# Second cross attention: the softmax matrix turned by VectorE blocks and device memory in place of TensorE

## The reference, cut to what matters

```python
def _L1_xattn_ref(query, key, value, w_q, w_k, w_v, w_o):   # key = value = ctx_1024 (8, 1024, 256)
    q = (query @ w_q).reshape(B, Q, HEADS, HEAD_DIM).transpose(0, 2, 1, 3)
    k = (key @ w_k)...; v = (value @ w_v)...
    scores = jnp.einsum('bhqd,bhkd->bhqk', q, k) * scale
    attn = jax.nn.softmax(scores, axis=-1)
    out = jnp.einsum('bhqk,bhkd->bhqd', attn, v)
    return out.transpose(0, 2, 1, 3).reshape(B, Q, HEADS * HEAD_DIM) @ w_o
x = x + _L1_xattn_ref(_layernorm(x, axis=-1), ctx_1024, ctx_1024, ...)
```

## Time and profile before

| what | us |
|---|---|
| median of 3 runs | 1009.84 |
| profiled execution, span from first to last instruction | 1008.6 |
| the stage changed (main loop and its tail) | 424 to 866 |
| one batch of 8 pairs in it | 52 |
| PE busy over the whole span | 963.9 |
| DVE, ACT, POOL busy over the whole span | 552.4, 497.9, 180.9 |

### The profile page before, as it was taken

How to read it: one execution, slowest core, us unless ns; L and a number is a source line. 1 busy time by engine, 2 the same in 40 slices (tenths; PEclk the granted TensorE clock), 3 DMA queues, 4 the chain that set the end, 5 groups by cost and what they waited for, 6 DMA issues and landing times. The chain is left out here.

```text
span 1008.6 us, 21010 instructions
## 1 busy us (share of the span) xinstructions
PE 963.9 (96%) x8772; PEld 798.4 (79%) x8772; DVE 552.4 (55%) x800; ACT 497.9 (49%) x716; POOL 180.9 (18%) x188
## 2 busy tenths in 40 slices
PE   8999999888899999899999999999999999997997
PEld 7888887665689985589999999998989996657554
DVE  5677777666443354565646465646464642367212
ACT  4777776353656645554444454454444532321331
POOL 2000000022224423012121212121212101421101
PEclk9999999899989999999999999999999999999999
DMA  5211110022023304111111111111113000599994
GB/s 154 86 47 47 47 47 5 2 63 65 2 84 94 94 22 167 37 48 43 43 43 42 42 42 42 42 42 42 42 58 140 0 1 1 133 332 310 336 328 143
DMA packets 57366, 84.55 MB, mean 84 GB/s; under 512 B 5506, under 2 KB 46163, under 8 KB 57299
## 3 DMA queue, kind: packets, MB, share of 16 engines
q1 hardware_dynamic: 56466, 81.22, 25.5%
q0 software_dynamic: 832, 2.36, 0.8%
HBM read 80.94 MB, written 2.62 MB: 83 GB/s over the span
## 5 line engine op out<-in xcount | busy, mean ns | idle before, releaser
L186 PE MATMUL ps<-f_pT_hi,f_cN_hi 128*128 128x256 f32 x512 | 145.4, 284 | 0.0
L186 PE MATMUL ps<-f_pT_hi,f_cN_lo 128*128 128x256 f32 x512 | 144.7, 283 | 0.0
L186 PE MATMUL ps<-f_pT_lo,f_cN_hi 128*128 128x256 f32 x512 | 144.7, 283 | 0.0
L1596 ACT ACTIVATE e_pr<-ps,e_negmax 128x1024 f32<-128x1024 f32 x64 | 71.5, 1116 | 129.9 <-DVE e_negmax L1601 127.6
L1870 DVE TENSOR_TENSOR f_pT_lo<-ps,f_pT_hi 128x1024 fp32r<-128x1024 f32 x64 | 78.3, 1224 | 81.8 <-ACT f_pT_hi L1808 81.6
L186 PE MATMUL ps<-e_cT_hi,e_qb_hi 128*128 128x512 f32 (+1 forms) x288 | 115.4, 401 | 0.0
L186 PE MATMUL ps<-e_cT_hi,e_qb_lo 128*128 128x512 f32 (+1 forms) x288 | 109.8, 381 | 0.0
L186 PE MATMUL ps<-e_cT_lo,e_qb_hi 128*128 128x512 f32 (+1 forms) x288 | 109.1, 379 | 0.0
L1808 ACT CAST f_pT_hi<-ps 128x1024 fp32r<-128x1024 f32 x64 | 64.9, 1014 | 84.6 <-PE ps L1920 83.8
L445 DVE SCALAR_TENSOR_TENSOR a_u<-ps,a_floor,a_cap 128x1024 f32<-128x1024 f32 x64 | 79.2, 1279 | 48.3 <-PE ps L540 47.9
L186 PEld LDWEIGHTS ps<-f_pT_hi,f_cN_hi 128*128 128x128 f32 x512 | 97.8, 191 | 2.6 <-issue 0.8
(11 more groups left out here) (401 smaller groups left out, 1961.0 us busy)
## 6 DMA issues: line engine op xcount, KB each, us to landing
k_w<-in_L_ffn_W SPq DMA_DIRECT2D x30, 1024.0 KB, 13.3
a_ctxT<-in_ctxT SPq DMA_DIRECT2D x16, 512.0 KB, 4.5
d_w<-in_L_ffn_w SPq DMA_DIRECT2D x32, 256.0 KB, 2.7
e_raw<-in_ctxT SPq DMA_DIRECT2D x8, 1024.0 KB, 5.0
e_raw<-in_ctx SPq DMA_DIRECT2D x8, 1024.0 KB, 5.8
k_b<-in_L_ffn_b SPq DMA_DIRECT2D x14, 256.0 KB, 11.8
k_w<-in_L_xattn_w_q SPq DMA_DIRECT2D x1, 1024.0 KB, 5.1
e_wk<-in_L_xattn_w_k SPq DMA_DIRECT2D x1, 1024.0 KB, 7.6
```

Of the source, the lines that this page charges most:

```text
L186: last = nc.tensor.matmul(out, a[i], b[j], start=start and n == 0, stop=stop and n == 2, skip_group_check=skip)
L1596: nc.scalar.activation(pr[:, p % NPR, :], core.ps[p % 2][:], ACT.Exp, bias=negmax[:, p:p + 1], accum_out=total[:, p:p + 1]).then_inc(exp_r ...
```

## The change

PE's transposes go. After the divide DVE turns each probability tile in 32x32 squares (`turn`, L1928 of the new kernel): within each block of 32 partitions, 32 columns become 32 partitions. What is missing is the exchange between blocks of partitions, and DMAs do it: SP stores the 128x1024 tile (512 KB) to a buffer in device memory (`put`, four slots) and fetches it back as four quarters (`fetch`), each into 32 partitions as 4 runs of 1 KB per partition. So a tile's context rows lie in another order, and the key loads follow that order (four DMAs per batch in place of one).

The fetched tile lands in `f_pT_lo`; ACT casts it to `f_pT_hi` (now from SBUF), and the low part overwrites the fetched tile: POOL makes that of the even pair of a group, DVE that of the odd one. Outputs read 256 columns as 2 x 4 runs of 32. The probabilities have no buffer of their own: they take the place of `xn` and `xnT`. `cT` is double-buffered; the cast of `cN` is cut by feature half; `wv` and `wo` take the place of `e_raw`; semaphores of the preparation are cleared on POOL. The loops over batches are written out in full: the PE program has 3716 listed rows where it had 2320. PE now runs scores of both pairs of group G and then the outputs of group G-2.

```diff
-        pr = core.sb("e_pr", [P, NPR, S], F32, ctx)
+        pr = [xn[:].rearrange("p j d -> p (j d)"), xnT[:].rearrange("p c n -> p (c n)")]
...
+                def put(n):
+                    sp.wait_ge(turned_ready, n + 1)
+                    if n >= SLOTS:
+                        sp.wait_ge(pT_in[n % 2], 64 * (n // 2 - 1))
+                    sp.dma_start(rows[n % SLOTS, :, :], turned[:, n % 2, :, :].rearrange("p j w -> p (j w)")
+                                 ).then_inc(rows_in[n % 2], 16)
+                def fetch(n):
+                    G = n // 2
+                    sp.wait_ge(rows_in[n % 2], 16 * (n // 2 + 1))
+                    if n >= 2:
+                        sp.wait_ge(pT_in[n % 2], 64 * (n // 2))
+                    if G >= 2:
+                        sp.wait_ge(o_psum, 2 * G - 2)
+                    for j in range(4):
+                        sp.dma_start(pT_lo[G % 2][QD * j:QD * j + QD, n % 2, :, :].bitcast(F32),
+                                     rows[n % SLOTS, :, S // 4 * j:S // 4 * (j + 1)].rearrange("(i k) w -> k i w", k=QD)
+                                     ).then_inc(pT_in[n % 2], 16)
+                for b, g in groups:
+                    G = NG * b + g
+                    put(2 * G)
+                    put(2 * G + 1)
+                    fetch(2 * G)
+                    fetch(2 * G + 1)
...
@@ scalar
+                for b, g in groups[1:]:
+                    G = NG * b + g
+                    if G >= 3:
+                        outputs(G - 3)
...
+                    exponentials(2 * G)
+                    high(2 * G - 2)
+                    exponentials(2 * G + 1)
+                    if g == 1 and b >= 1:
+                        keys(b, 0)
+                    high(2 * G - 1)
@@ vector
+                def turn(n):
+                    if n >= 2:
+                        dve.wait_ge(rows_in[n % 2], 16 * (n // 2))
+                    dve.wait_ge(p_ready, n + 1)
+                    nc.vector.transpose(turned[:, n % 2, :, :], pr[n % NPR].rearrange("p (j s) -> p j s", j=4)
+                                        ).then_inc(turned_ready, 1)
...
+                for b, g in groups[1:]:
+                    G = NG * b + g
+                    if G >= 2:
+                        low(2 * G - 3)
...
+                    for r in range(2):
+                        dve_maximum(dve, b, 2 * g + r)
+                    for r in range(2):
+                        dve_divide(dve, b, 2 * g + r)
+                        turn(2 * G + r)
@@ tensor
-                def transposes(b, p):
-                    for k in range(KT):
-                        last = nc.tensor.transpose(core.ps[2][:, k * P:(k + 1) * P],
-                                                   pr[:, p % NPR, k * P:(k + 1) * P], core.ident[:])
...
+                                        [t[G % 2][:, :, :, QD * m:QD * m + QD] for t in (pT_hi, pT_lo)],
...
+                for b, g in groups[1:]:
+                    G = NG * b + g
+                    for r in range(2):
+                        pe_scores(pe, b, 2 * g + r)
+                    if G >= 2:
+                        for c in range(DC):
+                            outputs(G - 2, c)
```

More of the change, by code:

```diff
@@ L1768, in _ @@
                 early.gpsimd()
[L1770 to L1774, removed]
-                                                ALU.subtract).then_inc(n_lo, 1)
[L1777 to L1780, removed]
+                nc.clear_and_free_semaphores(prepared)
@@ L1818, in attended, with queries @@
+                def queries(b, half):
+                    act.wait_ge(s_psum, HP * (b - 1) + HALF * (half + 1))
+                    act_queries(b, half)
                 def attended(p):
@@ L1862, in _ @@
+                act.wait_ge(v_in, 32)
+                nc.scalar.copy(wo2[0], wo).then_inc(wo_hi, 1)
+                outputs(LAST - 2)
+                attended(0)
+                attended(1)
+                high(2 * LAST)
+                outputs(LAST - 1)
+                high(2 * LAST + 1)
+                attended(2)
+                attended(3)
+                outputs(LAST)
+                for p in range(4, HP):
                     attended(p)
@@ L1976, in _ @@
-                transposes(0, 0)
-                pe_scores(pe, 0, 2)
-                each(pe, B, batch)
+                for b, g in groups[1:]:
+                    G = NG * b + g
+                    for r in range(2):
+                        pe_scores(pe, b, 2 * g + r)
+                    if G >= 2:
+                        for c in range(DC):
+                            outputs(G - 2, c)
+                pe.wait_ge(v_in, 32)
+                pe.wait_ge(exp_ready, HP * B)
+                values(0)
@@ L1979, in _ @@
+                values(1)
+                for c in range(DC):
+                    outputs(LAST - 1, c)
                 values(2)
                 values(3)
-                pe.wait_ge(pT_lo, HP * B)
-                pe.wait_ge(o_read, NG * B)
-                pe.wait_ge(wo_lo, 1)
-                for p in range(0, HP - 2, 2):
+                pe.wait_ge(wo_lo, 1)
+                pe.wait_ge(oT_dve, 2)
+                for p in range(2):
+                    for j in range(2):
+                        project(p, j)
```

314 lines of the change are left out of this document (148 added, 166 removed).

## The result

The changed kernel takes 993.9 us (median of 4 runs, 991.3 to 998.5) where the kernel before takes 1009.6 beside it: a ratio of 0.985 [0.983, 0.988], 16 us faster. Forecast were 964 and a gain of 46. The profiled execution took 992.0, its span is 990.0 where 962.4 was forecast, so 27.6 us are to be found. (Two small parts lie outside the span: the profiled execution took 2.0 more than its span, where the forecast had 1.2, and the median lies 1.9 above that execution.) Ratios are of fast executions alone, so one of run 7 (1133.3 us, at a granted clock of 0.74) and one of run 10 (979.9) stay out of them.

What follows compares the result with a forecast made beforehand. PE, busy all 52 us of a batch, was taken as the bound. -55.7 + 2.7 + 4.8 + 2.0 = -46.2 took the span from 1008.6 to 962.4; with 1.2 to the median, 963.6, forecast 964 us (958 to 976, chance 0.50).

Steps and rivals of the forecast that it cites:

- PE's own group: Scores and outputs of two pairs on PE without transposes: 2.77 + 2.87 = 5.64 us a pair, 11.28 a group.
- runs of 32 columns: Outputs on PE read 256 columns as 8 runs of 32, costed at nothing; a tenth wrong would cost 18 us.
- The start: Listing walked from 424.5 to group 3's scores at 446.5; PE idles 5.2 us there, 2.7 more than before.
- Turns: DVE's 32x32 transposes of a probability tile, taken at 1.22 us each, bounded by 0.75 and 2.33.
- store and quarters: SP's store and four fetches through device memory: 5.8 us, with ends 3.7 and 10.3.
- the links from the cast on: Cast, exponential, reciprocal and divide, wait for POOL, turn: 5.35 us without the DMA.
- I take 11.45 for the mean group, 0.17 over PE's: Mean group period, with context loads pushing some groups over PE's 11.28; costs 4.8 us over 28 groups.
- the chain at 11.15: Odd turn to odd turn through store, fetch, cast, exponential and divide: 11.15 us against PE's 11.28.
- rival B: DVE becomes the bound by turns of 2.33 or more locks with POOL: 986 us; chance 0.20, shared with longer chains.
- Values and projections move and cost the same: Tail of the stage, 831.63 to 864.09, only shifts; 2.0 us given for what is late at the end.
- A: DMA way is short and PE stays the bound in every group, 11.28 each: 958 us, chance 0.15.
- C: Round trip through device memory sets a long period: no gain at 13.1, 1045 us at 14.35; chance 0.12.

Runs made afterwards that it cites:

- run 7: The changed kernel with POOL's low part of 1024 columns written as two subtractions of 512: 1003.9 us, ratio 0.993.
- run 10: The changed kernel with both exponentials ahead of the casts on ACT and POOL's low part in halves, output weights not loaded early: 974.3 us, ratio 0.961.
- the control: The changed kernel measured once more, unedited, beside later variants: 998.6 us, ratio 0.987 against the kernel before.
- Run 5: The changed kernel with context and its transpose of batches 1 to 7 loaded in 16 columns, their values left out: 984.8 us, ratio 0.972.
- run 12: The changed kernel with both exponentials ahead of the casts, POOL's low part in halves and output weights loaded ahead of their group's stores, measured again: 967.7 us, ratio 0.958.
- run 4: The changed kernel with SP's order store even, fetch even, store odd, fetch odd instead of both stores first: 1043.1 us, ratio 1.033.
- run 3: The changed kernel with each fetched quarter as 1 KB of all 128 partitions, the exchange between blocks left out: 994.9 us, ratio 0.985.

## Why the prediction was wrong

**Right.** Direction and mechanism: the transposes go and a chain through DVE, DMA and ACT comes up to PE's pace. PE's own group, where it waits for nothing, is 11.25 to 11.32 (11.28 forecast). In it the 48 outputs with runs of 32 columns take 5.82 where two pairs took 5.74, 2 to 3 us over 32 groups, where I had put nothing. The start was walked to 446.5 for the scores of group 3 and came at 446.38; that it is so near is luck, since the control has 448.98. Turns take 1.25 (1.22), store and quarters 5.9 where nothing lies beside them (5.8), the links from the cast on 5.4 (5.35). No idle within the groups is put down to PE's sequencer, and what is put down to "issue" ends with DVE's low part, as shown above.

**The step that failed** is the term "I take 11.45 for the mean group, 0.17 over PE's". The working had the chain at 11.15 and knew of two things that lengthen it: it gave the context loads 0.3 and left the other, subtractions beside POOL, to rival B. The mean group took 12.03, so the chain exceeds PE's pace by 0.7 and not by 0.17. Per group the two are:

- *Context loads beside the way.* Kinds 3 and 0 take 1.09 and 0.91 more than kind 1: 0.50 per group in the mean, 14 us over 28. Run 5 takes them away and with them this part. The issues of before had 1 MB in 5.8 for such a load; in one queue with 2 MB of stores and fetches per group that was no small neighbour.
- *Subtractions beside POOL.* Kind 2 takes 0.80 more: 0.20 per group, 6 us. I priced the low part and the queries' part at 1.22 as if alone, while POOL subtracts for the features during them. This is rival B's rule, which I had weighed and left in a rival: SBUF — State Buffer of the Trainium skill (two separate sides) has a DVE operation with two SBUF inputs wait as the divide does. The trace agrees: 2.22 and 2.31 beside POOL, 1.18 and 1.22 alone. No run took this part away; it is read from the trace, and it is the same 12.1 in run 5.

Kind 1 alone gives 11.33, 0.12 under my 11.45: -3. Together 28 x (12.03 - 11.45) = 16; by the scores it is 28 x (12.13 - 11.45) = 19.0. The rest is that group 31's scores stand behind the outputs of group 28, which wait 2.3 and then take 7.33 where others take 5.82, at a granted clock of 0.77 in the mean:

```profile
778.77:786.10 7.33, 7.33 (x49) 7.33 (x50) 5.87 (x7) 4.38 (x6) 4.68 (x3) 0.77 0.86 220
```

The outputs of group 12 took the same 7.33 behind a wait of 2.2, those of group 24 only 5.84 behind one of 2.4. The sum of the prediction had no term for the clock.

**The tail, 6.4 us.** The forecast had 50.8 from the scores of group 31 (446.5 + 28 x 11.45 = 767.1) to the end of the stage (864.1 - 46.2 = 817.9); it took 57.2. "Values and projections move and cost the same" left out that their weights are loaded in SP's queue, now behind a fetch. PE waits 3.53 for them, and then the values begin at half speed:

```profile
801.04 5.44 PE L1999 MATMUL ps<-e_qc,e_raw 128*64 128x512 f32 x12 [3.53 <-DMA e_raw<-in_L_xattn_w_o]
```

This is 0.45 per matmul where the earlier trace rows have 0.23, and the granted clock of that stretch is 0.50, the level of 1.2 GHz:

```profile
801.00:806.50 5.50, 5.46 (x14) 1.88 (x16) 0.69 (x1) 2.97 (x3) 3.51 (x1) 0.50 0.64 178
```

That costs 2.7 us for these 12; with the wait it is 6.2 of the 6.4.

**After the stage** 2.2 us more (146.7 for 144.5), in code that did not change; no run was made on it. In the thirteen profiles of the changed kernel and its variants this stretch takes 143.1 to 151.1, so 2.2 may be no more than its spread. 19.0 + 6.4 + 2.2 = 27.6.

Of the rivals, A's group of PE's own 11.28 came near in kind 1 only (11.33). B's locks are real and cost less than B had as a whole (986). C's mechanism, a round trip that sets the period, is in part what happened, and showed in full in run 4. By SBUF — State Buffer of the Trainium skill (Door 1) C weighed narrow fetches too: the quarters into 32 partitions do land 0.7 later than wide ones (run 3), and the time is the same. The 964 that was forecast is nearly what the three edits of run 12 give (967.7), but that is another kernel and no support for the forecast.

## What to carry to other kernels

When a step is sent through device memory, list what the next iteration's work on each in-order engine waits for: here one cast that stood ahead of an exponential closed a loop over DVE, SP, DMA and ACT, and moving it one place gave as much again as the change itself. Price a round trip that lies on such a loop beside the loads that share its queue, not alone; and price every two-input SBUF operation of DVE at the time POOL may hold it. A load that stood in an idle queue is not free to keep its place when that queue gets waits.

## What the runs showed of the hardware

- A DVE turn of 128x1024 fp32 in 32x32 squares takes 1.25 us, the pace of its other full passes (1.21 to 1.23).
- A divide of DVE held by a POOL subtraction ends 0.55 after it; a DVE subtraction with both inputs in SBUF ends 1.1 after it (2.2 in place of 1.18), and the POOL subtraction that comes next takes 2.3 in place of 1.29. Where POOL's second half and the divide start at the same moment, the divide waits for that half too: 1.85 in place of 1.69 (run 7). POOL is held in the mean as well: `f_cN_lo` takes 1.62 where it took 1.29 before.
- Matmuls that read 256 columns as 8 runs of 32 cost 1 to 1.5% (5.82 for 48 against 5.74).
- PE can pay twice for a wait: after waits of 2.2, 2.3 and 3.5 us it ran on at a granted clock of 0.77, 0.77 and 0.50, which cost 1.5, 1.5 and 2.7 us more; after one of 2.4 it did not.
- A store of 512 KB lands in 3.5 us and a quarter of 128 KB in 3.4; with a fetch in front of the next store on one queue the same bytes cost 44 to 49 us more (run 4).
